# Mixing weights from a table in SBUF instead of fp32 kernel sums and a trip through DRAM

## What is computed

```python
h = gelu(cond_128 @ W0 + b0); h = gelu(h @ W1 + b1)
att = softmax(h @ W2 + b2)                      # 128 x 8
agg_w = einsum('bk,koi->boi', att, weight)      # one 64x64 kernel per batch
agg_b = att @ bias_k
y = einsum('boi,bih->boh', agg_w, x) + agg_b[:, :, None]
base = einsum('bsd,od->bso', y, base_W)
probs = softmax(y @ router_W.T); top 2 of 8, weights divided by their sum
mid = einsum('bsd,edr->bser', y, lora_A) * w_dense
out = x + base + 2 * einsum('bser,erd->bsd', mid, lora_B)
```

## Time and profile before

| | us |
|---|---|
| median of 3 runs | 992.72 |
| lowest and highest of the 3 | 991.69, 1067.75 |
| the profiled execution | 992.38 |
| its span, first to last instruction | 990.6 |

### The profile page before, as it was taken

The page is one execution under the profiler, slowest core; times in us unless marked ns, Lnnn a source line. Parts: engine busy times, 40 slices in busy tenths (PEclk is TensorE's granted clock), DMA queues, the critical chain, the costliest instruction groups (busy, mean ns, idle before and its releaser), DMA issues.

```text
span 990.6 us, 17707 instructions
## 1 busy us (share of the span) xinstructions
PE 963.9 (97%) x5742; PEld 882.8 (89%) x5742; DVE 686.5 (69%) x1529; ACT 208.7 (21%) x422; POOL 330.5 (33%) x245
## 2 busy tenths in 40 slices
PE   6788999999999999999999999999999999999998
PEld 4577999999999999999999999999999999999996
DVE  2878676677676667767667776766776766677674
ACT  3432121122211211212121121211212112122120
POOL 4904333322333322333332233333223333223331
PEclk9889999999999999999999999999999999999999
DMA  8324333433423333332343333334333233433311
GB/s 281 100 122 136 103 106 115 135 108 111 128 93 114 120 132 111 112 113 93 114 135 117 116 122 101 105 114 135 109 111 133 90 115 117 134 109 112 120 48 54
DMA packets 64145, 115.00 MB, mean 116 GB/s; under 512 B 38392, under 2 KB 38520, under 8 KB 63480
## 3 DMA queue, kind: packets, MB, share of 16 engines
q1 hardware_dynamic: 63856, 114.76, 35.0%
q10 hardware_dynamic: 272, 0.03, 0.0%
HBM read 79.01 MB, written 35.68 MB: 116 GB/s over the span
## 4 chain that ended last, share of the span: by engine, by line
PE 91%; issue 4%; POOL 2%; DMA 1%; DVE 1%; SPq 0%; POOLq 0%; DVEq 0%
PE pc L504 17%; PE pa L515 13%; PE pb L515 13%; PE y_ps L476 11%; PE pb L518 9%; PE pa L518 9%; PE pd L504 9%; PE pc L536 4%; PE pd L536 4%; DMA c_raw<-in_base_t 1%; PE pd L526 1%; POOL w_raw L360 1%; POOL w_raw L348 1%; POOL lb_lo L395 0%; DVE out_sb L910 0%
## 5 line engine op out<-in xcount | busy, mean ns | idle before, releaser
L405 POOL TENSOR_TENSOR out_sb<-out_sb,u 128x512 f32<-128x512 f32 x96 | 136.4, 1451 | 209.1 <-DVE u L956 209.1
L476 PE MATMUL y_ps<-mix_w,x_sb 128*128 128x128 f32 x1024 | 199.5, 280 | 0.7 <-issue 0.7
L476 PEld LDWEIGHTS y_ps<-mix_w,x_sb 128*128 128x128 f32 x1024 | 171.9, 194 | 17.3 <-issue 3.9
L366 POOL TENSOR_TENSOR ya<-ya 128x512 f32<-128x512 f32 x32 | 42.6, 1331 | 420.7 <-DVE ya L850 420.7
L850 DVE TENSOR_TENSOR ya<-y_ps,bias_sb 128x512 f32<-128x512 f32 x128 | 87.7, 686 | 34.4 <-PE y_ps L476 31.3
L504 PE MATMUL pc<-w_hi,s_hi 128*128 128x512 f32 x256 | 106.8, 417 | 2.9 <-DVE out_sb L910 2.9
L515 PE MATMUL pa<-w_hi,a_hi 128*128 128x376 f32 x256 | 101.5, 397 | 6.2 <-DVE w_lo L802 6.2
L504 PE MATMUL pc<-w_hi,s_lo 128*128 128x512 f32 x256 | 101.2, 395 | 0.0
L504 PE MATMUL pc<-w_lo,s_hi 128*128 128x512 f32 x256 | 100.5, 393 | 0.0
L515 PE MATMUL pa<-w_lo,a_hi 128*128 128x376 f32 x256 | 86.3, 337 | 0.0
L515 PE MATMUL pa<-w_hi,a_lo 128*128 128x376 f32 x256 | 86.2, 337 | 0.0
(11 more groups left out here) (149 smaller groups left out, 2373.6 us busy)
## 6 DMA issues: line engine op xcount, KB each, us to landing
x_sb<-in_x SPq DMA_DIRECT2D x64, 512.0 KB, 3.4
out_sb<-in_x SPq DMA_DIRECT2D x64, 512.0 KB, 4.3
out<-out_sb SPq DMA_DIRECT2D x64, 512.0 KB, 2.8
bias_sb<-bias_rows SPq DMA_DIRECT2D x62, 64.0 KB, 5.2
agg_rows<-agg SPq DMA_DIRECT2D x1, 2048.0 KB, 9.1
mix_w<-agg_rows SPq DMA_DIRECT2D x120, 16.0 KB, 3.3
a_raw<-in_base_t SPq DMA_DIRECT2D x1, 1024.0 KB, 7.8
c_raw<-in_base_t SPq DMA_DIRECT2D x1, 1024.0 KB, 12.4
```

The costliest lines, as they stand in the source:

```text
L366: nc.gpsimd.tensor_tensor(y_block(0, 1), y_block(0, 1), y_block(0, 0), ALU.subtract).then_inc(s3_set, 1)
L405: nc.gpsimd.tensor_tensor(o, o, u2[:, :], ALU.add).then_inc(done, 1)
L476: mm = nc.tensor.matmul(y_ps[q % 2][:, j * P:(j + 1) * P], x_sb[m][:, c * P:(c + 1) * P], mix_w[m][:, :], start=True, stop=True)
```

## The change

Every tile's mixing weights are now made on the core as those of pair 0 were. `mix_i` stays in SBUF for the whole kernel. A new table `att_rows` holds for each of the 64 tiles and each row the 8 attention values of the row's batch: VectorE spreads the attention (`att_spread`), one fp32 matmul with `parity` (128 x 512) makes the table, ScalarE copies it to SBUF. For each later tile POOL multiplies `mix_i` by the tile's columns of `att_rows` into `scaled` (`scale_mix`), VectorE reduces `scaled` into `summed[m]` (`sum_mix`), ScalarE places it in `mix_w[m]` with two copies (`place_mix`). There is one `scaled` for both tiles, so the second product waits for the first reduce. In the body of pair p this is done for pair p+2. `mixing_kernels`, `take_agg`, `agg`, `mix_k`, the DRAM copy and `mixing_weights` are gone. The bias of b2 comes with the parameters; the order of the first loads is changed (`mix_i` ahead of the first base block, the side columns ahead of the second x tile). `keep_warm` now issues 512-column fp32r matmuls of a one-hot table `hot` instead of 128-column transposes, 2, 1, 1, 3, 1 and 2 of them in place of 3, 1, 1 and 4.

```diff
@@ block.sync
             sp.dma_start(mlp[:, :], params).then_inc(params_in, 16)
+            sp.dma_start(mix_i[:, :], mix_t).then_inc(mix_i_in, 16)
+            sp.dma_start(bk_sb[:, :], bias_k).then_inc(bk_in, 16)
             sp.dma_start(a_raw[:, :], base_t[0, :, :]).then_inc(a_in, 16)
-            for b in range(PAR):
-                sp.dma_start(mix_i[b * C:(b + 1) * C, :], mix_t).then_inc(mix_i_in, 16)
...
-            sp.dma_start(mix_k[:, :], mix_rows).then_inc(mix_k_in, 16)
...
             def load_x(n, m):
                 next_x(n, m)
-                mixing_weights(2 * n + m, m, agg_dram)
                 mixing_bias(2 * n + m, m)
...
-            sp.dma_start(agg_dram.ap(), agg[:, :]).then_inc(agg_out, 16)
@@ block.gpsimd
+            def scale_mix(n, m):
+
+                if first(n - 1 if isinstance(n, int) else n):
+                    pool.wait_ge(att_rows_set, 1)
+                pool.wait_ge(summed_set, 2 * n + m)
+                nc.gpsimd.tensor_tensor(scaled[:, :].rearrange("p (c k) -> p c k", k=K),
+                                        mix_i[:, :].rearrange("p (c k) -> p c k", k=K),
+                                        att_rows[:, bass.ts(2 * n + m, K)].unsqueeze(1).broadcast_to(
+                                            [P, C, K]), ALU.mult).then_inc(scaled_set, 1)
+
             make_t1(0)
             sums(0)
             make_t1(1)
+            scale_mix(1, 0)
             make_t2(0)
+            scale_mix(1, 1)
             make_t2(1)
...
                 add_u2(p, k)
+                mixes = not (isinstance(p, int) and p >= NP - 2)
+                if mixes:
+                    pool.wait_ge(u2_in21, p + 1)
+                    scale_mix(p + 2, 0)
                 if not last(p):
                     sum_s2(p + 1)
+                if mixes:
+                    scale_mix(p + 2, 1)
+                if not last(p):
                     sums_s1_s4(p + 1)
@@ block.tensor
-            pe.wait_ge(mix_k_in, 16)
-            mixing_kernels(0)
+            keep_warm(1)
...
                 for j in range(HALF):
                     mix_chunk(0, q, j)
-                if q < 3:
-                    mixing_kernels(q + 1)
+                if q == 1:
+                    pe.wait_ge(spread_set, 1)
+                    nc.tensor.matmul(pb[:, BANK:], parity[:, :], att_spread[:, :], start=True,
+                                     stop=True).then_inc(att_rows_mm, 1)
@@ block.scalar
-            def place_mix(m):
-
-                act.wait_ge(zeros_set, 4)
-                act.wait_ge(summed_set, m + 1)
+            def place_mix(n, m):
+
+                act.wait_ge(summed_set, 2 * n + m + 1)
+                if first(n):
+                    act.wait_ge(zeros_set, 4)
+                else:
+                    act.wait_ge(mixed, 4 * n + m - 1)
...
                     split_high(A12, p + 1, y_ready, 4 * p + 8)
+                mixes = not (isinstance(p, int) and p >= NP - 2)
+                if mixes:
+                    place_mix(p + 2, 0)
                 exponents(2 * p + 1)
+                if mixes:
+                    place_mix(p + 2, 1)
@@ block.vector
+            def sum_mix(n, m):
+
+                dve.wait_ge(scaled_set, 2 * n + m + 1)
+                if not first(n):
+                    dve.wait_ge(mix_set[m], PAR * n)
+                nc.vector.tensor_reduce(summed[m][:, :], scaled[:, :].rearrange("p (c k) -> p c k", k=K), AX.X,
+                                        ALU.add).then_inc(summed_set, 1)
...
                 add_p5(p, k)
+                mixes = not (isinstance(p, int) and p >= NP - 2)
+                if mixes:
+                    sum_mix(p + 2, 0)
                 add_side_b(p)
                 add_up11_p74(p, k)
+                if mixes:
+                    sum_mix(p + 2, 1)
```

More of the change, by code:

```diff
@@ L112, in adaln_ffn_kernel @@
         _, warm = place("warm", 1)
+        _, mix_i = place("mix_i", C * K)
+        _, att_rows = place("att_rows", NT * K)
+        summed = [place(f"summed{m}", C)[1] for m in range(2)]
         assert top[0] <= 229344
@@ L256, in mixing_bias @@
                              bias_dram.rearrange("s (t r) -> t s r", t=NT)[t, :, :].partition_broadcast(P)
[L257 to L265, removed]
-                    else:
-                        src = agg_dram[r, :].rearrange("(i s c) -> i s c", i=C, s=2)
-                    sp.dma_start(dst[:, :, b, :], src).then_inc(mix_w_in[m], 16)
+                             ).then_inc(bias_in[m], 16)
             def next_x(n, m):
@@ L288, in _ @@
                 next_x(1, m)
-            sp.wait_ge(agg_mm, NA)
             load_residual(0, 0)
-            sp.wait_ge(agg_act, NA)
-            for m in range(2):
-                mixing_weights(2 + m, m, agg)
             sp.wait_ge(bias_out, 16)
@@ L421, in keep_warm @@
                 for _ in range(times):
-                    nc.tensor.transpose(pb[:, 0:P], ident[:, :], ident[:, :])
-            def mixing_kernels(n):
-                if n == 4:
-                    pe.wait_ge(scaled_set, 2)
-                elif n == 5:
-                    pe.wait_ge(bias_set, 2)
-                elif n >= 6:
-                    pe.wait_ge(agg_act, n - 3)
-                nc.tensor.matmul(agg_ps[n], att_t[:, :], mix_k[:, n * BANK:(n + 1) * BANK],
-                                 start=True, stop=True).then_inc(agg_mm, 1)
+                    nc.tensor.matmul(pb[:, 0:BANK], hot[:, 0:P], hot[:, :], start=True, stop=True)
+            pe.wait_ge(hot_set, 1)
             pe.wait_ge(consts_set, 1)
-            keep_warm(3)
+            keep_warm(2)
             pe.wait_ge(params_in, 16)
@@ L566, in body @@
                     up(1, pc, True, up22_mm)
-                else:
-                    for n in range(4, NA):
-                        mixing_kernels(n)
                 wait_operand(A12, p)
@@ L732, in _ @@
             split_high(A11, 0, y_ready, 2)
-            take_agg(2)
-            take_agg(3)
+            act.wait_ge(att_rows_mm, 1)
+            nc.scalar.copy(att_rows[:, :], pb[:, BANK:]).then_inc(att_rows_set, 1)
             split_high(A12, 0, y_ready, 4)
@@ L745, in first_body @@
                     take_hi(T3, n)
-                for n in range(4, NA):
-                    take_agg(n)
+                place_mix(1, 0)
                 for n in range(WP):
```

104 lines of the change are left out of this document (55 added, 49 removed).

## The result

The changed kernel took 1066.97 us (median of 4, 1066.13 to 1067.12), the kernel before 993.0 us (median of 4). The ratio is 1.0748, 95% interval 1.0727 to 1.0769: 7.5% slower. One of the four runs of the kernel before was in a slower state of the chip (1067.75 us) and is left out of the ratio, which compares 1066.97 with 992.72. The profiled execution took 1066.13 us.

A forecast was written before the change was run, and what follows sets the result against it. The prediction took PE, busy with matmuls throughout the body, to bound the kernel. From 992.4 us it added 75 for new body waits and subtracted 5 for the start: 1062 us, range 1005 to 1110.

The forecast's parts named there:

- What bounds the kernel, and where it is decided: Body: PE's matmuls bound it; the chain behind a pair's second routing, done before PE runs out of matmuls, decides.
- POOL's product at 1.28: Body: each added POOL product takes 1.28 us, the time of s2, starting 0.08 behind the last u2 addition.
- the rival of 2.2 (1116 us): Body: POOL's product costs 2.2 us, 129 us in all, giving 1116 us; chance 0.08.
- Turns: `ties` and the product of ties held, 2.4 us: Second routing: VectorE operations take turns with POOL's, each of these some 1.2 us instead of 0.2; `mid` ends 2.4 late.
- The rival in which `ties` slips through: Second routing: `ties` goes with `beats` before POOL's s1; 1.7 us per pair, 1038 us; chance 0.23, a quarter near 1005.
- The wait at the transpose, 1.4 us: Second tile's `mid` transpose: PE waits 1.4 us per pair for VectorE's addition that frees `pd`.
- The wait at the up product, 1.1 us: Up product: PE waits 1.1 us per pair for mid_lo, behind reduce, placing, splits of s2 and s1, and mid_hi.
- Per pair 2.5, 75 us in all: Body: PE waits 2.5 us per pair, not won back, over pairs 0 to 29: 75 us; bounds 18 and 129.
- The removed transfers, nothing: Body: removing the 120 transfers of 16 KB gains nothing, as PE doesn't wait for them.
- The start, 5 us: Start: first A11 product 7.4 us earlier, less 2.6 for POOL and 0.6 for VectorE; 5 gained, bounds 0 and 8.
- The rival of 1110: Body: PE's clock falls in every pair after the waits, 48 us more, 1110 us; chance 0.08.
- Not slower: Body: PE's cover holds, second tile's `mid` done by 143.05, only the start counts: 987 us; chance 0.11.

The follow-up runs named there:

- e_none: The changed kernel with no POOL products, VectorE reduces or ScalarE placings from pair 2 on, later tiles using pair 1's weights: 985.17 us.
- e_pool: The changed kernel with only the POOL products kept from pair 2 on, reduces and placings left out: 1032.23 us.
- e_quarter: e_pool with each POOL product cut into four pieces of 128 columns: 1013.37 us.
- e_act: The changed kernel, whole computation, with ScalarE placing the second tile's weights later, behind mid_hi of the next body: 1042.98 us.
- e_gap3: e_gap2 with the first pair's products and sums placed like the other pairs', sums ahead of the first make_u2: 987.08 us, 0.994 of the kernel before.
- e_gap2: e_gap with products written into s2's and s1's places, sums behind additions of p12 and p5, placings behind the split of A12: 991.92 us, ratio 0.9996.
- e_gap: The changed kernel with both POOL products behind S3, both sums ahead of make_u2, both placings ahead of mid_hi: 1002.91 us, ratio 1.0109.

## Why the prediction was right, step by step

- **What bounds the kernel, and where it is decided.** Held. e_none shows PE free of waits without the added work, and the two waits in the body of the changed kernel are the two that were named, at the transpose behind VectorE's addition into out_sb and at the up product behind mid_lo.
- **POOL's product at 1.28.** Measured 1.28 to 1.30 in the body, so the rival of 2.2 (1116 us) fell. It starts 0.28 behind the last addition and not 0.08, and side_b is 0.66 late instead of 0.5; the operations of POOL behind it follow 1.24 to 1.25 apart, a little closer than reckoned, so that `pd` is free 9.04 us behind the last addition (forecast 9.11).
- **Turns: `ties` and the product of ties held, 2.4 us.** Both took the 1.2 to 1.3 us forecast. e_pool shows the effect without any added VectorE work, and e_quarter that the length of the POOL instruction sets it. The rival in which `ties` slips through is refuted by the row of `ties` (1.32).
- **The wait at the transpose, 1.4 us.** From the end of the last addition of u2 to the transpose it is 9.20 us (138.37 to 147.57), before 7.72: 1.48. The transpose starts 0.16 behind the end of VectorE's addition, which the sum had at nothing. The profile records the wait as 1.3.
- **The wait at the up product, 1.1 us.** From the transpose to the up product it is 3.39 us instead of 2.26: 1.13. It is the chain of reduce, placing, splits and mid_hi that was forecast; e_act takes 0.80 of it away.
- **Per pair 2.5, 75 us in all.** Measured 2.59 in each pair of the body, so the step that was worked out is right to 0.1. The total was 82 us, and the rest is not in the body: the first pair was taken to be like the others at 2.5 and lost 6.1 (35.28 against 29.19), with the wait of 3.2 and the low clock behind it; 1.1 was lost ahead of it, and the last pair that prepares another lost 1.2. With 72.5 in the body that makes 81. The first pair's loss is one of order: in e_gap3, with the products and sums elsewhere, it lasts 29.25 us.
- **The removed transfers, nothing.** Nothing contradicts it: e_none is without them too and gains only what the start gives; they weren't put back alone.
- **The start, 5 us.** Measured 6.9 (e_none), within the bounds of 0 and 8, but its two terms were both off. The head was to bring the first A11 product 7.4 us forward; it came 11.8 forward. The sum let the mixing matmuls of pair 0 take as long as before, and they took 2.60 and 2.05 us for 16 each, instead of 2.0 to 2.1 for 8. The granted clock is 1.00 in both, so the profile doesn't say why. Against this, 2.6 + 0.6 was reckoned for POOL and VectorE ahead of w_lo; from the first A12 product to the first T2 product 7.8 us of the lead were lost. That 5 came near 6.9 is in part luck. 5.7 of the 6.9 is the lead at the first T2 product. The rest comes behind: after the wait for w_lo the granted clock was 0.50 until 64 us in the kernel before, 4.2 us from 59.83 on, and until some 57 us in e_none, 3 us from 54.11 on; and a wait of 0.65 us at 85.29 us of the kernel before is missing.
- **The sum, 1062.** Measured 1067. 7 us too little lost and 2 too little gained partly cancel.
- **The clock.** The rival of 1110 fell. The granted clock in the body is 1.00 with waits of 1.32 and 0.83 us in each pair, and 0.50 came only in the first pair, behind the waits of 2.96 (up to 72.30 us) and 3.20; the Trainium skill's case (TensorE: Matmul & The Clock Gate, "HAM oscillation — how this bites in real kernels"), cold anew in every tile, didn't come about here.
- **Not slower.** It fell as the changed kernel stands, and on its own terms: all that is added stood ahead of `mid`. With the same work elsewhere (e_gap3) nothing is lost in the body; that it took 987.08 us where this rival said 987 is chance, as the start gained 6.9 in e_none and not 5.

## What to carry to other kernels

Before an engine with idle time is given more work, look at which short operations of its partner run at that moment: a POOL operation of 1.3 us put beside a chain of 0.2 us VectorE operations costs the chain over 1 us per operation, and the busy shares show it as work. Place such work where its neighbours are long or have slack, and give each product a buffer of its own that is dead there, so that no wait ties the order; here that turned 1.075 into 0.994, with the same work in the body. A delay is also cheap only as long as the chain behind it has slack: the same placing cost 0.3 us a pair at most without the products and 0.8 with them. And a pair that is written out by hand needs the same care as the loop, in the sum as well as in the code: in e_gap2 the first pair alone took back 5 of the 7 us that the start gains, and in the changed kernel it lost 6.1 us where the forecast had 2.5.

## What the runs showed of the hardware

- Copies and scalar operations of fp32 are held by POOL too, and not only those with two SBUF inputs: in e_quarter `gate` took 0.82 us beside POOL's s4 (0.23 alone, in e_gap3), and in e_gap `chosen` took 0.84 (0.17 alone) beside POOL's first product (125.31 to 126.6):

```profile
125.78 0.84 DVE L897 TENSOR_SCALAR chosen<-rank 128x8 f32<-128x8 f32 x1
126.74 1.12 DVE L903 TENSOR_TENSOR picked<-exps,chosen 128x8 f32<-128x8 f32 x1
```

  By the Trainium skill (SBUF — State Buffer, "Who interferes with whom") such operations can take part; the trace agrees. What the runs add is the length: each waits for the end of the POOL instruction that it meets, one for one, however short the operation itself.
- Four POOL products of 128 columns took 1.72 us, one of 512 columns 1.29: the pieces cost 0.43 more, and e_quarter was still 18.9 us faster than e_pool.
- An operand that is repeated over 64 groups by a stride of zero costs POOL nothing: the product took 1.29 us, as did the addition s2.
- TensorE's recorded wait of 1.35 us in e_pool stands where 1.57 us were lost from one start to the next, and a pair of its body lasts 1.53 us longer. The ends of matmuls are modelled, so a loss is better read from one start to the next.
